# A gated cross-attention and FFN kernel: key projection of the next group ahead of the attention output, late gate loads, and a float32 FFN for the last two groups

## The chip, the cores and the metric

The kernel runs on one core of one Trainium2 chip, as one launch. The metric is the device time of one execution in microseconds. The median before is 78.19 us over three executions.

## The reference

Sixteen batches of 128 rows with 256 features go through one gated attention block and one gated feed-forward block. Cut to what matters:

```python
# x, ctx: (16, 128, 256); mask: (16, 128); all float32
q = layernorm(x) @ Wq.T + bq
k = ctx @ Wk.T + bk
s = where(mask, -inf, q @ k.T)            # per batch, 128 x 128
o = softmax(s) @ ctx                      # the values are ctx itself
x1 = x + tanh(g_xattn) * (o @ Wo.T + bo)
w = (W_ffn >= 0) * 2 - 1                  # signs only
y = clip((layernorm(x1) @ w.T) * scale + bias, -100, 100)
out = x1 + tanh(g_ffn) * y
```

## The kernel before

The sixteen batches are taken as G = 8 groups of GB = 2; L = 7 is the last group. A batch's 128 rows are the partitions and the 256 features are DC = 2 chunks of 128. The two query and key weights are multiplied once into one 256 x 256 product (`multiply_weights`, names `ps_wqk`, `wqk_hi`, `wqk_lo`), so that a group needs only one projection of ctx, called K, against the transposed normalised x. Wo with the gate in it is likewise applied to ctx before the attention, as Z, so that softmax(s) @ Z is already the projected output O.

A group g goes through these steps. TensorE transposes x (`transpose_x`), ctx (`transpose_ctx`) and later x1 (`transpose_x1`). ScalarE evicts the transposed ctx rounded to float32r (`cT_hi`), and VectorE subtracts that from the original to get the rest (`cT_lo`); K and Z are made of three float32r products for each chunk (hi x hi, lo x hi, hi x lo). Scores S are float32. VectorE adds the mask and takes the minimum (`mask_and_min`), ScalarE does the exponential (`exp`), TensorE transposes it (`transpose_p`), ScalarE evicts it, and `attend` multiplies it by Z in float32. VectorE's `residual` divides and adds x with the bias, giving x1. Its statistics (`stats_x1`), its reciprocal standard deviation (`rstd_of_x1`, GpSimd) and its transposed hi and lo halves (`evict_x1T_hi` on ScalarE, `split_x1T` on VectorE) lead to `ffn`, which is eight float32r matmuls of 256 columns for a group. The mean is taken out of the FFN weights (`w_mid`, `wT`). VectorE then scales (`scale_y`), GpSimd adds the bias (`add_bias`), and VectorE clips and adds x1 (`clip_and_add`).

Each engine has its order written out by hand; engines meet by semaphores only, and a wait blocks all that stands behind it on its engine. TensorE's order for group i in the loop is K(i), transposed x1(i-1), Z(i), S(i), transposed ctx(i+1), half of F(i-1), transposed p(i), the other half of F(i-1), transposed x(i+1), O(i). After the loop `finish_last` does the last group with its two batches staggered over spare PSUM banks. The last FFN has hi and lo halves too (`split_last_x1T`), and VectorE finishes it in four steps of two batches each (`scale_last_y`, `add_last_bias`, `clip_last`, `add_last_x1`), behind one addition for the whole of group L-1.

All loads are issued by SP in one order: x(0), Wq, Wk, ctx(0), Wo, x(1), ctx(1), mask, bo, x(2), W_ffn, ctx(2), and so on, each of 256 KB or 128 KB. ScalarE's queue issues bq, bk and the two gates at once at the start. TensorE runs float32 matmuls on zeros (`warm_up`) while it has nothing to do; in the order stand 6, then bq and bk transposed, 3, the gates spread over the partitions, 2, and then the product of weights. ScalarE's first activation is tanh of the gates, and its activation table is loaded ahead of that.

Of the kernel before, what the change touches and what calls it, by code (L numbers as in the profile page):

```python
# [19 lines left out]
def gated_xattn_ffn(nc, x, ctx, mask, g_xattn, g_ffn, wq, bq, wk, bk, wo, bo, w_ffn, scale_ffn, bias_ffn, out):  # L20
# [20 lines left out]
    with ExitStack() as stack:  # L41
# [6 lines left out]
        def bank(name):  # L48
# [12 lines left out]
        last_O, last_F = [ps_O[:, 0], k_bank[:, 0:D]], [ps_F[:, 0], z_bank[:, 0:D]]  # L61
# [29 lines left out]
        wT = sb("wT", [P, DC, D], F32R)  # L91
# [10 lines left out]
        ps_gates = xT_bank[:, 0:2]  # L102
# [15 lines left out]
            sem(n) for n in ("ps_wqk_ready", "wqk_hi_ready", "wqk_lo_ready", "ps_u_ready", "u_ready"))  # L118
        ve_last_done, eps_ready = sem("ve_last_done"), sem("eps_ready")
# [20 lines left out]
        dve_biased_done = sem("dve_biased_done")  # L140
# [5 lines left out]
        def _(sp):  # L146
# [10 lines left out]
            sp.dma_start(wo_sb[:], wo.rearrange("(c p) d -> p c d", p=P)).then_inc(wo_loaded, 16)  # L157
            load_x(1)
            load_ctx(1)
            sp.dma_start(mask_u8[:], mask.rearrange("(o b) k -> o b k", o=1).to_broadcast([P, B, P])  # L160
                         ).then_inc(mask_loaded, 16)
            sp.dma_start(bo_sb[:], bo.rearrange("(o d) -> o d", o=1).to_broadcast([P, D])).then_inc(bo_loaded, 16)
            load_x(2)
# [9 lines left out]
            for g in range(L):  # L173
                if g == L - 2:
                    sp.wait_ge(pool_out_done, GB)
                else:
                    sp.wait_ge(out_done, g + 1 if g < L - 2 else g)
                sp.dma_start(out_rows[:, rows(g), :], out_sb[:, rows(g), :]).then_inc(stored, 16)
            for b in range(GB):
                sp.wait_ge(out_done, L - 1 + b + 1)  # L180
                sp.dma_start(out_rows[:, L * GB + b, :], out_sb[:, L * GB + b, :]).then_inc(stored, 16)
            sp.wait_ge(stored, 16 * (G + 1))

        @block.scalar
        def _(act):
            for k, v in enumerate((bq, bk)):
                act.dma_start(vec_rows[k * DC:(k + 1) * DC, :], v.rearrange("(c p) -> c p", p=P)).then_inc(vecs_loaded, 16)
            for k, v in enumerate((g_xattn, g_ffn)):
                act.dma_start(gate_row[:, k:k + 1], v.rearrange("(o d) -> o d", o=1)).then_inc(gates_loaded, 16)
# [43 lines left out]
            def evict_last_x1T_hi(b):  # L233
                act.wait_ge(x1T_prod, L + b + 1)
                nc.scalar.copy(x1T_hi[:, L % 2, :, b * P:(b + 1) * P], last_x1T[b]).then_inc(x1T_hi_done, 1)
# [9 lines left out]
            for m in range(DC):  # L245
                act.wait_ge(ps_K0_ready, m + 1)
                nc.scalar.activation(K_sb[:, 0, m], ps_K0[m], ACT.Identity, bias=u_col[:, m:m + 1]).then_inc(K_done, 1)  # L247
            act.wait_ge(ps_woT_ready, 1)
            act.wait_ge(tanh_ready, 1)
            nc.scalar.activation(woT_hi[:], by_chunk(z_bank), ACT.Identity, scale=tanh_g[:, 0:1]).then_inc(woT_hi_ready, 1)  # L250
            evict_cT_hi(1)
# [4 lines left out]
            act.wait_ge(w_mean_ready, 1)  # L256
            for c in range(DC):
                nc.scalar.activation(w_mid[:, c], w_sign2[:, c], ACT.Identity, bias=w_mean[:, c:c + 1]).then_inc(w_mid_ready, 1)
            for i in range(1, G + 1):
                if i < G:  # L260
                    evict_K(i)
                if i < G:
                    evict_x1T_hi(i - 1)
                    if i == 1:
                        act.wait_ge(ps_wT_ready, 1)
                        nc.scalar.copy(wT[:], ps_wT).then_inc(wT_ready, 1)
# [546 lines left out]
```

## Time and profile before

| | before |
|---|---|
| median of three executions | 78.19 us (78.17 to 80.32) |
| the profiled execution, its time | 78.39 us |
| its span, first to last instruction | 76.6 us |
| granted TensorE clock, mean over the span | 0.984 |
| TensorE matmul busy | 68.9 us (90%) |
| VectorE busy | 58.9 us (77%) |
| GpSimd busy | 54.7 us (71%) |
| ScalarE busy | 43.2 us (56%) |

The span is that of the profiled execution; 1.8 us of its time lie outside the span. Busy time counts compute only. In the rows further down, PE is TensorE's matmuls (PEld its weight loads), DVE is VectorE, ACT is ScalarE, POOL is GpSimd and SP is SyncE; SPq and ACTq are an engine issuing a DMA. L610 and the like are lines of the kernel. A float32 matmul shows as two records, a float32r matmul as one.

### The profile page before, as it was taken

What the parts mean: (1) busy time and instruction counts of PE and PEld (TensorE: products, weight loads), DVE (VectorE), ACT (ScalarE), POOL (GpSimd) and SP (SyncE); (2) the same over time, 40 slices, a digit from 0 to 9 for tenths busy, and PEclk for the clock granted to TensorE, in tenths of its full rate; (3) what the DMA queues carried; (4) which work ended last, traced back from release to release, by engine and by line L of the source; (5) the groups of instructions that cost most, each with busy time, mean ns of one, the idle gap of its engine ahead of it and who ended that gap; (6) DMA issues with size and microseconds to landing.
All of it is one profiled execution on the core that took longest, in us unless ns stands there. A gap on an engine that the chain in (4) does not pass through costs nothing.

```text
span 76.6 us, 1617 instructions
## 1 busy us (share of the span) xinstructions
PE 68.9 (90%) x513; PEld 64.1 (84%) x513; DVE 58.9 (77%) x186; ACT 43.2 (56%) x118; POOL 54.7 (71%) x111
## 2 busy tenths in 40 slices
PE   4999998989999999999999999999999999975400
PEld 4989997969999999999989999999999899943300
DVE  0191692799437999999899998989877987489980
ACT  0600626775997199619943993597379716726000
POOL 4057008898988998998988798689869338998500
PEclk9999999999999999999999999999999999999985
DMA  0979999999910000040012004000400040012214
GB/s 8 287 223 322 264 248 317 323 368 349 327 56 5 4 4 0 9 137 0 0 42 95 0 0 137 9 0 0 137 0 0 0 137 12 0 59 78 78 59 137
DMA packets 8229, 8.10 MB, mean 106 GB/s; under 512 B 537, under 2 KB 8093, under 8 KB 8221
## 3 DMA queue, kind: packets, MB, share of 16 engines
q1 hardware_dynamic: 8208, 8.00, 33.4%
q8 instruction: 4, 0.07, 0.4%
q14 instruction: 5, 0.03, 0.2%
q10 hardware_dynamic: 12, 0.00, 0.0%
HBM read 5.90 MB, written 2.10 MB: 104 GB/s over the span
## 4 chain that ended last, share of the span: by engine, by line
PE 86%; DVE 4%; ACT 3%; POOLq 1%; issue 1%; POOL 1%; DVEq 0%
PE ps_Z L610 15%; PE ps_K L610 14%; PE ps_S L610 12%; PE ps_F L610 10%; PE ps_O L685 8%; PE ps_xT L605 8%; PE ps_F L730 7%; PE ps_cT L605 5%; PE ps_S L677 3%; POOLq L41 1%; PE ps_O L610 1%; PE ps_O L710 1%; DVE y_biased L484 1%; DVE y_clip L489 1%; ACT Z_sb L215 1%
## 5 line engine op out<-in xcount | busy, mean ns | idle before, releaser
L362 POOL TENSOR_TENSOR xb_sb<-x_sb,bo_g 128x256 f32<-128x256 f32 x16 | 12.9, 829 | 0.6
L367 POOL TENSOR_TENSOR y_biased<-y_scaled,bias_g 128x256 f32<-128x256 f32 x14 | 10.2, 734 | 3.8 <-DVE y_scaled L504 3.8
L210 ACT ACTIVATE K_sb<-ps_K,u_col 128x256 f32<-128x256 f32 x14 | 5.9, 470 | 10.9 <-PE ps_K L610 10.9
L610 PE MATMUL ps_Z<-woT_hi,cT_hi 128*128 128x256 f32 x32 | 9.7, 303 | 0.0
L610 PE MATMUL ps_K<-cT_hi,wqk_hi 128*128 128x256 f32 x30 | 9.7, 323 | 0.0
L610 PE MATMUL ps_F<-wT,x1T_hi 128*128 128x256 f32 x30 | 8.9, 320 | 0.8 <-DVE x1T_lo L472 0.8
L610 PE MATMUL ps_Z<-woT_hi,cT_lo 128*128 128x256 f32 x32 | 9.1, 283 | 0.0
L610 PE MATMUL ps_Z<-woT_lo,cT_hi 128*128 128x256 f32 x32 | 9.0, 283 | 0.0
L610 PE MATMUL ps_S<-K_sb,xT 128*128 128x128 f32 x64 | 8.5, 276 | 0.2 <-ACT K_sb L247 0.2
L610 PE MATMUL ps_K<-cT_hi,wqk_lo 128*128 128x256 f32 x30 | 8.5, 282 | 0.0
L610 PE MATMUL ps_K<-cT_lo,wqk_hi 128*128 128x256 f32 x30 | 8.4, 282 | 0.0
L300 POOL TENSOR_SCALAR ve_x<-mv_x 128x2 f32<-128x2 f32 x8 | 3.1, 386 | 7.2 <-DVE mv_x L412 7.1
L610 PEld LDWEIGHTS ps_S<-K_sb,xT 128*128 128x128 f32 x64 | 7.8, 192 | 0.4 <-issue 0.4
L409 DVE BATCH_NORM_STATS2 bn_x<-x_sb 128x6 f32<-128x256 f32 x16 | 5.9, 408 | 2.5 <-DMA x_sb<-in_x_dram 2.5
L610 PE MATMUL ps_F<-wT,x1T_lo 128*128 128x256 f32 x30 | 7.8, 282 | 0.0
L685 PE MATMUL ps_O<-Z_sb,PT_sb 128*128 128x256 f32 x28 | 7.3, 383 | 0.3 <-ACT PT_sb L227 0.3
L504 DVE SCALAR_TENSOR_TENSOR y_scaled<-ps_F,rstd,scale_g 128x256 f32<-128x256 f32 x14 | 6.5, 474 | 0.7 <-PE ps_F L610 0.7
L424 DVE TENSOR_TENSOR cT_lo<-ps_cT,cT_hi 128x512 fp32r<-128x512 f32 x8 | 5.5, 683 | 1.8 <-ACT cT_hi L193 1.8
L448 DVE SCALAR_TENSOR_TENSOR x_sb<-ps_O,recip_p,xb_sb 128x256 f32<-128x256 f32 x14 | 6.1, 479 | 0.9 <-PE ps_O L685 0.8
L200 ACT ACTIVATE xn<-x_sb,nmr_x,rstd_x 128x256 f32<-128x256 f32 x12 | 6.6, 612 | 0.0
L221 ACT ACTIVATE p_sb<-t_sb,smin 128x128 f32<-128x128 f32 x16 | 6.3, 396 | 0.4 <-DVE smin L437 0.3
L610 PEld LDWEIGHTS ps_F<-wT,x1T_hi 128*128 128x128 f32 x30 | 5.7, 188 | 1.0 <-issue 1.0
(129 smaller groups left out, 206.1 us busy)
## 6 DMA issues: line engine op xcount, KB each, us to landing
x_sb<-in_x_dram SPq DMA_DIRECT2D x8, 256.0 KB, 6.7
ctx_sb<-in_ctx_dram SPq DMA_DIRECT2D x8, 256.0 KB, 6.8
out_dram<-out_sb SPq DMA_DIRECT2D x7, 256.0 KB, 2.1
wq_sb<-in_L_xattn_Wq_dram SPq DMA_DIRECT2D x1, 256.0 KB, 3.0
wk_sb<-in_L_xattn_Wk_dram SPq DMA_DIRECT2D x1, 256.0 KB, 4.3
wo_sb<-in_L_xattn_Wo_dram SPq DMA_DIRECT2D x1, 256.0 KB, 5.2
mask_u<-in_mask_BxS_bk_dram SPq DMA_DIRECT2D x1, 256.0 KB, 6.5
w_sb<-in_L_ffn_weights_dram SPq DMA_DIRECT2D x1, 256.0 KB, 7.8
```

The source lines that it names most:

```text
L200: nc.scalar.activation(xn[:, r], x_sb[:, r], ACT.Identity, scale=rstd_x[:, r:r + 1], bias=nmr_x[:, r:r + 1]).then_inc(xn_done, 1)
L210: nc.scalar.activation(K_sb[:, g % 2, m], ps_K[:, m], ACT.Identity, bias=u_col[:, m:m + 1]).then_inc(K_done, 1)
L221: nc.scalar.activation(p_sb[:, g % 2, b], t_sb[:, g % 2, b], ACT.Exp, scale=-1.0, bias=smin[:, r:r + 1], accum_out=psum_p[:, r:r + 1]).the ...
L362: nc.gpsimd.tensor_tensor(xb_sb[:, r], x_sb[:, r], bo_g[:], ALU.add).then_inc(xb_done, 1)
L367: nc.gpsimd.tensor_tensor(y_biased[:, g % 2, b], y_scaled[:, g % 2, b], bias_g[:, 0], ALU.add).then_inc(biased_done, 1)
L409: nc.vector.bn_stats(bn_x[:, g * GB + b], x_sb[:, g * GB + b]).then_inc(bn_x_done, 1)
L424: nc.vector.tensor_tensor(cT_lo[:, g % 2], ps_cT, cT_hi[:, g % 2].bitcast(F32), ALU.subtract).then_inc(cT_lo_done, 1)
L448: nc.vector.scalar_tensor_tensor(out=x1_sb[:, r], in0=ps_O[:, b], scalar=recip_p[:, r:r + 1], in1=xb_sb[:, r], op0=ALU.mult, op1=ALU.add). ...
L504: nc.vector.scalar_tensor_tensor(out=y_scaled[:, g % 2, b], in0=ps_F[:, b], scalar=rstd_1[:, r:r + 1], in1=scale_g[:], op0=ALU.mult, op1=A ...
L605: last = nc.tensor.transpose(dst[:, c, b * P:(b + 1) * P], src[:, b, c * P:(c + 1) * P], ident[:])
L610: last = nc.tensor.matmul(dst, lhsT, rhs, start=(n == 0), stop=(n == len(pairs) - 1))
L685: last = nc.tensor.matmul(ps_O[:, b], PT_sb[:, g % 2, b], Z_sb[:, g % 2, b], start=True, stop=True)
```

## The change

Seven edits are in it.

1. SP loads Wq, Wk, ctx(0) ahead of x(0), the mask ahead of x(1), and x(2) ahead of bo. ScalarE's queue waits for ctx(0) before it issues the two gate loads.
2. In the prologue the gates' matmul and the two warm-up matmuls behind it are gone from their place. The gates' matmul now stands behind the first half of K(0); x(0) is transposed behind it and the second half of K(0) behind that. ctx(1) is transposed ahead of S(0). VectorE takes the statistics of x(0) behind `wq_neg`.
3. In the loop TensorE's order is K(i), transposed x(i+1), O(i-1), S(i), transposed ctx(i+1), transposed x1(i-1), Z(i), transposed p(i), F(i-1). The other engines' orders follow it; statistics of x are taken three groups ahead.
4. `clip_and_add` is cut in two with `scale_y` between the halves.
5. GpSimd multiplies the FFN weights by the gated scale (`wT_scaled`), a half each in groups 3 and 4.
6. Groups L-1 and L have a float32 FFN on those weights, without hi and lo halves: one ScalarE copy of the transposed x1 and, for each batch, two float32 matmuls of 256 columns. VectorE then multiplies by the standard deviation and adds the bias in one instruction.
7. TensorE's tail is interleaved batch by batch, and the group L-1 is clipped, added and stored last of all.

```diff
-            load_x(0)
             sp.dma_start(wq_sb[:], wq.rearrange("(c p) d -> p c d", p=P)).then_inc(wq_loaded, 16)
             sp.dma_start(wk_sb[:], wk.rearrange("(c p) d -> p c d", p=P)).then_inc(wk_loaded, 16)
             load_ctx(0)
+            load_x(0)
...
+            act.wait_ge(ctx_loaded[0], 16)
             for k, v in enumerate((g_xattn, g_ffn)):
                 act.dma_start(gate_row[:, k:k + 1], v.rearrange("(o d) -> o d", o=1)).then_inc(gates_loaded, 16)
...
-            act.wait_ge(ps_gates_ready, 1)
-            nc.scalar.activation(tanh_g[:], ps_gates, ACT.Tanh).then_inc(tanh_ready, 1)
             act.wait_ge(ps_wqk_ready, 1)
             nc.scalar.copy(wqk_hi[:, 0], ps_wqk[0]).then_inc(wqk_hi_ready, 1)
...
+            act.wait_ge(ps_K0_ready, 1)
+            nc.scalar.activation(K_sb[:, 0, 0], ps_K0[0], ACT.Identity, bias=u_col[:, 0:1]).then_inc(K_done, 1)
+            act.wait_ge(ps_gates_ready, 1)
+            nc.scalar.activation(tanh_g[:], ps_gates, ACT.Tanh).then_inc(tanh_ready, 1)
...
+            for i in range(1, L):
+                evict_K(i)
...
+                evict_xT(i + 1)
+                exp(i)
+                evict_x1T_hi(i - 1)
...
+                evict_cT_hi(i + 1)
+                if i + 2 < G:
+                    normalise_x(i + 2)
+                evict_Z(i)
+                evict_PT(i)
...
+            for i in range(1, L):
+                residual(i - 1)
+                mask_and_min(i)
                 stats_x1(i - 1)
...
                 split_x1T(i - 1)
...
+                split_cT(i + 1)
+                if i >= 2:
+                    clip_y(i - 2)
+                scale_y(i - 1)
+                if i >= 2:
+                    add_x1(i - 2)
+                if i + 3 < G:
+                    stats_x(i + 3)
...
+                nc.gpsimd.tensor_tensor(wT_scaled[:, c], wT[:, c].bitcast(F32), scale_g[:], ALU.mult
+                                        ).then_inc(wT_scaled_ready, 1)
...
             for i in range(1, L):
                 project_K(i)
+                if i == 1:
+
+                    attend(0)
+                    transpose_x(2)
+                else:
+                    transpose_x(i + 1)
+                    attend(i - 1)
+                scores(i)
+                transpose_ctx(i + 1)
                 transpose_x1(i - 1)
...
                 project_Z(i)
...
+                ffn(i - 1)
             project_K(L)
+            attend(L - 1)
+            scores(L)
+            project_last_Z(0)
             transpose_x1(L - 1)
+            transpose_p(L)
+            project_last_Z(1)
+            attend_last(0)
+            ffn_before_last(0)
+            attend_last(1)
+            transpose_last_x1(0)
+            ffn_before_last(1)
+            transpose_last_x1(1)
+            last_ffn(0)
+            last_ffn(1)
...
+                nc.vector.scalar_tensor_tensor(out=y_biased[:, L % 2, b], in0=last_F[b], scalar=rstd_1[:, r:r + 1],
+                                               in1=bias_g[:, 0], op0=ALU.mult, op1=ALU.add).then_inc(last_biased_done, 1)
```

## Rows read from the trace of the kernel before

**Rows 1.** Windows over three of the loop's groups: length, busy time (count) by engine, clock.

```profile
25.20:32.61 7.41, 7.41 (x60) 6.91 (x60) 7.26 (x22) 5.04 (x14) 6.75 (x14) 1.00 0.01 4
32.61:39.91 7.30, 7.30 (x61) 6.90 (x60) 7.04 (x22) 5.03 (x14) 6.71 (x12) 1.00 0.11 36
...
54.52:61.80 7.28, 7.28 (x60) 7.00 (x60) 6.06 (x17) 5.03 (x14) 4.66 (x9) 1.00 0.10 35
```

**Rows 2.** Chain that ended last, one group: start, duration, engine, tile, line, records.

```profile
56.38 1.44 PE ps_Z L610 x12
...
60.49 0.44 PE ps_xT L605 x4
60.93 0.87 PE ps_O L685 x4
```

**Rows 3.** The same chain, the prologue.

```profile
5.74 0.38 PE ps_xT L744 x2
...
6.76 0.87 PE ps_S L610 x4
...
10.15 0.82 PE ps_K L610 x6
...
12.35 1.13 PE ps_S L610 x8
...
15.49 0.58 ACT Z_sb L215
...
16.38 1.10 PE ps_O L685 x4
```

**Rows 4.** Timeline of SP's queue: the third and the fourth load, start and duration.

```profile
1.72 0.46 SPq L155 DMA_DIRECT2D wk_sb<-in_L_xattn_Wk_dram  x1
...
2.22 0.53 SPq L151 DMA_DIRECT2D ctx_sb<-in_ctx_dram  x1
```

**Rows 5.** DMA issues, those two alone: KB each, us from issue to landing.

```profile
wk_sb<-in_L_xattn_Wk_dram SPq DMA_DIRECT2D x1, 256.0 KB, 4.3
...
ctx_sb<-in_ctx_dram SPq DMA_DIRECT2D x1, 256.0 KB, 4.8
```

**Rows 6.** Timeline of ScalarE at the start: its last gate load and the table load.

```profile
1.87 0.27 ACTq L189 DMA_DIRECT2D gate_row<-in_g_ffn_dram  x1
...
2.18 1.28 ACT L238 ACT_TABLE_LOAD   x1 [2.18 <-issue]
```

**Rows 7.** Timeline of VectorE and GpSimd: x(0) from its landing to normalised.

```profile
3.48 0.75 DVE L409 BATCH_NORM_STATS2 bn_x<-x_sb 128x6 f32<-128x256 f32 x2 [2.50 <-DMA x_sb<-in_x_dram]
...
6.39 1.09 POOL L314 TENSOR_SCALAR xn<-x_sb,rstd_x,nmr_x 128x256 f32<-128x256 f32 x2
```

**Rows 8.** Groups by form: count, busy us, mean ns, idle before.

```profile
L221 ACT ACTIVATE p_sb<-t_sb,smin 128x128 f32<-128x128 f32 x16 | 6.3, 396 | 0.4 <-DVE smin L437 0.3
...
L514 DVE TENSOR_TENSOR out_sb<-y_clip,x_sb 128x512 f32<-128x512 f32 x5 | 5.5, 1104 | 0.2
...
L231 ACT CAST x1T_hi<-ps_xT 128x512 fp32r<-128x512 f32 x7 | 4.1, 586 | 0.0
```

**Rows 9.** The chain again, where the scores of the last group have ended.

```profile
65.98 0.95 PE ps_F L610 x8
```

**Rows 10.** Groups by form in the tail, VectorE.

```profile
L589 DVE TENSOR_TENSOR out_sb<-y_clip,x_sb 128x512 f32<-128x512 f32 x1 | 0.7, 680 | 0.0
...
L489 DVE TENSOR_SCALAR y_clip<-y_biased,lim 128x256 f32<-128x256 f32 x2 | 0.7, 404 | 0.0
...
L479 DVE SCALAR_TENSOR_TENSOR y_scaled<-ps_F,rstd,scale_g 128x256 f32<-128x256 f32 x1 | 0.5, 483 | 0.0
```

**Rows 11.** Timeline of VectorE, its last two instructions.

```profile
73.56 0.75 DVE L495 TENSOR_TENSOR out_sb<-y_clip,x_sb 128x256 f32<-128x256 f32 x2
```

**Rows 12.** DMA view, the stores of the output: KB each, median us to landing.

```profile
out_dram<-out_sb SPq DMA_DIRECT2D x7, 256.0 KB, 2.1
...
out_dram<-out_sb SPq DMA_DIRECT2D x2, 128.0 KB, 1.8
```

More of the change, by code:

```diff
@@ L250, in _ @@
             nc.scalar.activation(woT_hi[:], by_chunk(z_bank), ACT.Identity, scale=tanh_g[:, 0:1]).then_inc(woT_hi_ready, 1)
+            act.wait_ge(ps_K0_ready, DC)
+            nc.scalar.activation(K_sb[:, 0, 1], ps_K0[1], ACT.Identity, bias=u_col[:, 1:2]).then_inc(K_done, 1)
             evict_cT_hi(1)
@@ new lines, in _ @@
+            evict_K(L)
+            exp(L)
+            act.wait_ge(x1T_prod, L)
+            nc.scalar.copy(x1T_whole[:], ps_xT).then_inc(x1T_hi_done, 1)
+            evict_PT(L)
+            act.wait_ge(Z_prod, L + 2)
+            nc.scalar.copy(Z_sb[:, L % 2, 1], last_Z[1]).then_inc(last_Z_done[1], 1)
+            for b in range(GB):
+                act.wait_ge(x1T_prod, L + b + 1)
+                nc.scalar.copy(xT[:, 0, :, b * P:(b + 1) * P], last_x1T[b]).then_inc(x1T_hi_done, 1)
+                r = L * GB + b
+                act.wait_ge(mv_1_done, r + 1)
+                nc.scalar.activation(ve_1[:, r:r + 1], mv_1[:, r, 1:2], ACT.Identity, bias=eps_col[:, 0:1]
+                                     ).then_inc(ve_last_done, 1)
@@ L501, in scale_y @@
                 dve.wait_ge(F_prod, g + 1)
-                for b in batches:
+                for b in range(GB):
                     r = g * GB + b
@@ L686, in attend, with ffn @@
                 last.then_inc(O_prod, 1)
-            def ffn(g, batches):
+            def ffn(g):
                 pe.wait_ge(x1T_lo_done, g + 1)
@@ L693, in ffn @@
                     pe.wait_ge(wT_ready, 1)
-                for b in batches:
+                for b in range(GB):
                     pairs = []
@@ new lines, in ffn, with project_last_Z @@
+                last.then_inc(F_prod, 1)
+            def project_last_Z(b):
+                pe.wait_ge(Z_done, L)
+                if b == 1:
+                    pe.wait_ge(K_done, DC * G)
+                pairs = []
+                for c in range(DC):
+                    c_hi, c_lo = (t[:, L % 2, c, b * P:(b + 1) * P] for t in (cT_hi, cT_lo))
+                    pairs += [(c_hi, woT_hi[:, c]), (c_hi, woT_lo[:, c]), (c_lo, woT_hi[:, c])]
+                accumulate(last_Z[b], pairs).then_inc(Z_prod, 1)
@@ new lines, in ffn_before_last, with attend_last @@
+            def ffn_before_last(b):
+                pe.wait_ge(x1T_hi_done, L)
+                pe.wait_ge(wT_scaled_ready, DC)
+                pe.wait_ge(scaled_done, GB * (L - 1))
+                last = accumulate(ps_F[:, b], [(x1T_whole[:, c, b * P:(b + 1) * P], wT_scaled[:, c]) for c in range(DC)])
+                if b == GB - 1:
+                    last.then_inc(F_prod, 1)
+            def attend_last(b):
+                pe.wait_ge(last_Z_done[b], 1)
+                pe.wait_ge(PT_done, GB * L + b + 1)
+                if b == 0:
+                    pe.wait_ge(x1_done, GB * L)
+                nc.tensor.matmul(last_O[b], PT_sb[:, L % 2, b], Z_sb[:, L % 2, b], start=True, stop=True
+                                 ).then_inc(O_prod, 1)
@@ new lines, in transpose_last_x1, with last_ffn @@
+            def transpose_last_x1(b):
+                pe.wait_ge(x1_done, GB * L + b + 1)
+                for c in range(DC):
+                    last = nc.tensor.transpose(last_x1T[b][:, c], x1_sb[:, GB * L + b, c * P:(c + 1) * P], ident[:])
+                last.then_inc(x1T_prod, 1)
+            def last_ffn(b):
+                pe.wait_ge(x1T_hi_done, L + b + 1)
+                pe.wait_ge(wT_scaled_ready, DC)
+                accumulate(last_F[b], [(xT[:, 0, c, b * P:(b + 1) * P], wT_scaled[:, c]) for c in range(DC)]
+                           ).then_inc(F_prod, 1)
```

292 lines of the change are left out of this document (109 added, 183 removed).

## The prediction, made before the change was run

> **What bounds the kernel now.** I read the windows over the loop's groups first. In the last of three shown TensorE is busy 7.28 us of 7.28, in the first 7.41 of 7.41 [rows 1]: it has no hole, so a reordering can take nothing out of a group. VectorE is nearly as full, 7.26 of 7.41 and 7.04 of 7.30 us in the groups that also carry the statistics of a later x and the final add; without the statistics it is at 6.06 of 7.28 [rows 1]. So a new wait on VectorE of more than 0.2 to 0.3 us lengthens such a group. The chain that ended last says the same: one TensorE piece after another, each at a fixed price [rows 2]. Only the two ends are left to win something: the prologue up to the first O, where TensorE once stands behind ScalarE's evictions of Z and p [rows 3], and the tail behind the scores of the last group, which end at 65.98 [rows 9], 76.6 - 65.98 = 10.6 us before the end.
>
> **Start.** The product of weights starts at 6.76; the gates' matmul starts at 5.74 and it and the warm-up behind it are all that lies between [rows 3], so the product can start about 1.0 us sooner, at 5.74, if Wk is there. The third load in the queue lands at 1.72 + 4.3 = 6.0 and the fourth at 2.22 + 4.8 = 7.0 [rows 4, 5]. Wk is now second and so surely there by 6.0, ctx(0) is third (6.0), x(0) fourth (7.0, not first). What was won is then waited away, by two chains.
>
> Chain A is x(0). From the first look at x(0), 3.48, to its last normalised row, 6.39 + 1.09 = 7.48, are 4.0 us [rows 7], and that latency moves with the load: 7.0 + 4.0 = 11.0. Before, it ended at 7.48 and was hidden under the weights; now it is behind them. Behind it stand: x(0) transposed, 0.44 [rows 2]; the second half of K(0), half of a 12-record projection, 0.72 [rows 2]; the gates' matmul in front of it all, up to 0.38 [rows 3]; and ScalarE's eviction of half of K with two hand-overs, for which I take 0.6 (an eviction of 512 columns is 0.59, of 128 columns 0.40 [rows 8]). With half of the gates' price that is 11.0 + 0.2 + 0.44 + 0.72 + 0.6 = 13.0 for the first scores.
>
> Chain B is ScalarE. Its gate loads wait for ctx(0), 6.0; two issues take 0.6 (one is 0.27, and the table load began 0.31 after the start of the last [rows 6]); and the table load of 1.28 us stands behind them in its order, since it comes ahead of the first activation [rows 6]. Before, that was over at 3.46, in idle time. Now it would run 6.6 to 7.9, and the first eviction of the product waits for it, though the product is ready at about 6.6. From the product's first half (7.63) to K(0) (10.15) were 2.5 us [rows 3], so K(0) starts at 10.4 at the latest and its half ends at 11.1 or 11.2, about when x(0) is ready. So B is hidden by A, with nothing to spare. The product at 5.74 could also meet the clock at 1.2 GHz rather than 2.4: twice its 0.87 [rows 3] still ends before 7.9. Bounds for the first scores: 12.4 (loads that land 0.6 sooner) and 13.4 (the full gates' price and 0.2 for each chain's hand-overs); I take 13.0, against 12.35 before [rows 3].
>
> The scores are 0.65 later. But ctx(1) is already transposed, -0.44 (as [rows 2]), and K(1) now lies ahead of O(0), in the place where TensorE waited for the evictions of Z and p. From Z(0)'s end, just before 15.49, to the end of that O, 16.38 + 1.10 = 17.48, are 2.0 us [rows 3], and the work in it is 0.44 (p), 0.44 (x) and 0.87 (O) [rows 2] = 1.75 at the most: -0.3. Start in all: +0.65 - 0.44 - 0.3 = **-0.1** (from -0.7 to +0.3).
>
> **Loop.** TensorE does the same pieces. Their prices don't change, and the five groups took 7.28 to 7.41. The new order has one thin place. F(i-1) needs the low half of x1, which VectorE computes when ScalarE has evicted the high half; and ScalarE does that behind both exponentials. From the start of `mask_and_min` this is about 0.3 + 2 x 0.40 + 0.59 = 1.7 us [rows 8], or 1.8 with the reads of the sums between. VectorE arrives there sooner, at 0.6 (two masks) + 0.9 (two statistics) = 1.5 us, my reading from half-lengths of the same kind (0.75 for two statistics [rows 7]), and stands idle for 0.3. Added to its 7.04 us of work [rows 1] this is 7.34, 0.06 above TensorE's 7.28. That concerns groups 2, 3 and 4, which carry both the statistics of x and the final add: 3 x 0.06 = 0.2. The others have 1 us to spare on VectorE. Before, the first groups lost 0.15 to 0.2 as well (7.41 against 7.28). I take **+0.1**; the bounds are 0 and +1.0, which is 0.33 for three groups: 7.26 [rows 1] + 0.35. Splitting clip and add costs nothing by itself, as it is the same two instructions; the two scalings of weights on GpSimd (about 0.8 us each by the same shape) fall in groups 3 and 4, where it is busy 6.7 of 7.3 [rows 1], and what they delay there (bias and norm of a later x) has about 1 us of slack; without that cover they cost 0.2 each.
>
> **Tail.** Counted from the end of the last scores, TensorE now does Z(7) 1.44, x1(6) transposed 0.44, p(7) 0.44, O(7) 0.87, F(6), x1(7) transposed 0.44, and F(7). Four records of float32 with 256 columns take 0.87 (O), thus 0.44 for a matmul [rows 2]; the float32r FFN of a group was 0.95 [rows 9]. In float32 it is four matmuls, 1.74: the change makes TensorE 0.8 us slower in each of the two groups, and pays it for the VectorE split between. The sum is 1.44 + 0.44 + 0.44 + 0.87 + 1.74 + 0.44 + 1.74 = 7.1 us, without a hole as the batches are interleaved and every eviction (0.4 to 0.6 [rows 8]) has 0.7 or more of other work over it. F of the first batch is ready at 7.1 - 0.87 = 6.2. VectorE then needs 0.48 + 0.40 + 0.40 for a batch, now one dependent chain, and twice: 6.3 + 1.3 + 1.3 = 8.9; and the add of the whole group 6, 0.68, comes last: 9.6 [rows 10]. From VectorE's last result, 73.56 + 0.75 = 74.31 [rows 11], to the end were 2.3 us; the last store is now 256 KB and not 128 KB, 2.1 against 1.8 [rows 12], so 2.6. The tail is 12.2 us against 10.6, +1.6. But Z(7) and x1(6) transposed, 1.88 together, came before the last scores and now come behind: **-0.3** (-0.6 without the larger store and with a free group add; +0.4 if VectorE's instructions stretch beside GpSimd's clips as the add did, 1.10 against 0.68 [rows 8, 10]).
>
> **Sum.** -0.1 + 0.1 - 0.3 = -0.3 us on a span of 76.6. The profiled execution is 78.39, 0.2 above the median; so the median goes from 78.19 to **77.9 us**.
>
> **Two rules of the Trainium skill against this.** The trace has the table load at 1.28 us with nothing in front of or behind it that waits [rows 6]. ScalarE: Activation LUTs in the Trainium skill, section What ACT_TABLE_LOAD costs, has the same 1283 ns and adds about 1380 ns of drain; this trace can't show it, and by it chain B would end 1.4 us later and the median be near 79.1. The final add on VectorE took 1.10 us in the loop and 0.68 in the tail [rows 8, 10]. The page Perfetto Trace Analysis of the Trainium skill, section Optimizing Scalar/DVE Operations, says that GpSimd and VectorE share an SBUF read port; the trace agrees with it, and it speaks for the slower rival below.
>
> **The rivals.**
> - *The table load holds ScalarE longer than its own row.* The activation behind it starts up to a second 1.28 later. Chain B then sets the start: first scores at 14.2 to 14.3, the rest as above, 77.9 + 1.2 = 79.1. For it: the load has been moved out of idle time. Against: in the trace nothing stood behind it, so nothing shows such a cost.
> - *The loop waits on VectorE.* This is the side of slower. F(i-1) waits for the low half of x1 in every group, because VectorE's adds stretch beside GpSimd; VectorE is at 7.26 + 0.35 = 7.6 [rows 1], 0.3 for each of the six groups, +1.8: 79.6. It decides from 0.05 for a group on: 6 x 0.05 eats the 0.3 of the forecast. For it: the first group of before, 7.41. Against: the later groups carry less.
> - *The start is really shorter.* Loads land sooner with x(0) out of the way, and the table load runs in ScalarE's wait for ctx(0), so neither chain holds TensorE; the 1.0 us of warm-up is won whole, first scores at 12.0: 76.9. For it: the warm-up stood on the path. Against: 4.0 us of latency of x(0) [rows 7] don't go away.
> - *The float32 FFN gives nothing back.* The tail is as long as the sum of both, 77.9 + 0.8 = 78.7; it needs a hole in TensorE's tail of 0.8, and all operands are ready earlier in my walk.
>
> **Chances.** Forecast 0.50, table load 0.12, VectorE's loop 0.14, shorter start 0.18, tail 0.06. The forecast's own range is 77.2 to 78.6 (start and tail at their bounds against each other). With the rivals the range is 76.7 to 79.3: it leaves out half of the loop's case and a third of the short start. About 2% is what a measurement of this kernel can tell from no change, 76.6 and 79.8. Faster than that needs the short start and a good tail (0.12); slower needs the loop's case beyond 79.6 or two of them (0.09).
>
> **What would show it.** In the profile after: x(0) normalised at about 11 and the first scores at 13.0; a table load at 6.6 that ends at 7.9, and the distance of the next activation from it; windows over a group at 7.3 us with TensorE full; a wait of TensorE in front of F for `x1T_lo` if the loop's case holds; four float32 FFN matmuls at 1.74 for groups 6 and 7; and some 12.2 us from the end of the last scores to the end. The prediction is wrong first of all if the loads don't land in the order and at the times of their slots.

## The result, and the profile after

| | before | after |
|---|---|---|
| median | 78.18 us (78.00 to 80.32) | 80.02 us (79.05 to 82.72) |
| ratio to before, 95% interval | | 1.0134 (1.0086 to 1.0182) |
| the profiled execution, its time | 78.39 us | 79.05 us |
| its span | 76.6 us | 77.2 us |
| granted TensorE clock, mean | 0.984 | 0.982 |

Two of the four executions of after (80.76 and 82.72) had a lower mean granted clock (0.965 and 0.950); the ratio leaves these two and the slow one of before (80.32) out, and by it the change costs 1.0 us, where the forecast was a gain of 0.3. Two repetitions in later sessions, on two chips, gave 1.0108 (1.0011 to 1.0205) and 1.0059 (1.0016 to 1.0101). So the change makes the kernel some 0.5 to 1 us longer; in the two profiles the span is 0.6 us longer.

The chain that ended last, of after, from the third load to O(0), and two pieces of group 1 behind it, S(1) and F(0) (start, duration, engine, tile, line, records). The names are those of the PSUM banks: ps_O at 11.21 is the gates' matmul, ps_F at 12.18 the second half of K(0), and ps_S with two records the transposed p.

```profile
1.71 4.33 DMA ctx_sb<-in_ctx_dram
...
6.33 4.84 DMA gate_row<-in_g_ffn_dram
...
11.21 0.38 PE ps_O L779 x2
11.59 0.59 PE ps_xT L614 x4
12.18 0.73 PE ps_F L619 x6
...
13.55 1.13 PE ps_S L619 x8
...
18.21 0.87 PE ps_O L694 x4
...
19.52 1.12 PE ps_S L619 x8
...
23.60 0.95 PE ps_F L619 x8
```

The first scores start at 13.55, against 12.35 before [rows 3], and neither x(0) nor the table load is in the chain: it is the load of the second gate, one number, which ScalarE issued at 6.33, with SP's loads of 256 KB under way, and which landed at 11.17. ScalarE's timeline shows the table load beside it:

```profile
6.63 1.28 ACT L239 ACT_TABLE_LOAD   x1 [6.63 <-DMA ctx_sb<-in_ctx_dram]
7.92 0.37 ACT L239 CAST wqk_hi<-ps_S 128x256 fp32r<-128x256 f32 x1
```

Windows over two of the loop's groups of after, the partners of [rows 1]:

```profile
24.55:31.91 7.36, 7.36 (x61) 7.04 (x60) 5.74 (x20) 5.02 (x17) 6.12 (x13) 1.00 0.02 4
...
53.94:61.28 7.34, 7.34 (x61) 7.03 (x60) 5.49 (x17) 4.36 (x14) 4.80 (x8) 1.00 0.11 36
```

A group takes 7.34 to 7.36 us. TensorE looks full, but VectorE is at 5.5 to 5.7 in these two and at 6.3 to 6.4 in the three groups between them, not at 7. The view of waits says what TensorE's full time hides (who <- for whom: us in total, times, longest):

```profile
DVE x1T_lo L452 <- ACT x1T_hi L236: 1.9, 6, 0.3
...
PEld ps_F L619 <- DVE x1T_lo L452: 1.0, 5, 0.2
```

And the end of the chain, from the last group of the loop on (cf. [rows 9]):

```profile
59.88 0.22 PE ps_S L686 x2
60.10 1.18 PE ps_F L619 x8
61.28 1.44 PE ps_K L619 x12
62.72 0.87 PE ps_O L694 x4
63.59 0.11 issue
63.70 1.13 PE ps_S L619 x8
...
70.14 0.88 PE ps_S L619 x4
```

F(5) has 1.18 where F took 0.95 before [rows 9]; in front of the scores of group 7 TensorE stands; and the last piece shown, which is the FFN of the first batch of group 7 (it lies in the bank of the scores), ends at 71.02.

**Where the time went.** I cut both spans at the same work. To the end of K(1) and O(0): before 17.49 + 1.43 = 18.9 (O(0) from [rows 3], a K as in the loop), after 19.08: +0.2. From there to the start of K(7), which is 61.80 before [rows 1] and 61.28 after, are 42.9 before; less the O(6) that the new order does later, 0.87 [rows 2], that is 42.0, against 42.2 after: +0.2. From there to the end: before 14.8 with that O added 15.7, after 15.9: +0.25. Sum +0.6, the difference of the spans.

### The profile page after: what moved, and what is told of

Same layout as the page of the kernel before. It is cut to its first block, busy times and chain, and to the rows that moved or that the text cites. A ratio compares the mean times of both kernels' runs of the same rounds, so it can differ in the third digit from the quotient of the medians.

```text
span 77.2 us, 1595 instructions
## 1 busy us (share of the span) xinstructions
PE 69.7 (90%) x509; PEld 65.1 (84%) x509; DVE 55.9 (72%) x182; ACT 42.4 (55%) x118; POOL 54.5 (71%) x111
## 4 chain that ended last, share of the span: by engine, by line
PE 76%; DMA 12%; DVE 3%; issue 2%; SPq 1%; DVEq 1%; ACT 1%; ACTq 0%
PE ps_K L619 14%; PE ps_Z L619 14%; PE ps_F L619 12%; PE ps_S L619 11%; PE ps_xT L614 9%; PE ps_O L694 8%; DMA gate_row<-in_g_ffn_dram 6%; DMA ctx_sb<-in_ctx_dram 6%; PE ps_cT L614 3%; PE ps_S L686 2%; DVE y_biased L497 1%; DVE y_clip L500 1%; PE ps_O L733 1%; DVEq L41 1%; ACT K_sb L252 1%
## 5 line engine op out<-in xcount | busy, mean ns | idle before, releaser
L382 POOL TENSOR_TENSOR y_biased<-y_scaled,bias_g 128x256 f32<-128x256 f32 x12 | 9.4, 802 | 0.2
L619 PE MATMUL ps_Z<-woT_hi,cT_hi 128*128 128x256 f32 x30 | 9.1, 304 | 0.0
L619 PE MATMUL ps_K<-cT_hi,wqk_hi 128*128 128x256 f32 x30 | 8.7, 289 | 0.5 <-DVE wqk_lo L547 0.5
L619 PE MATMUL ps_Z<-woT_hi,cT_lo 128*128 128x256 f32 x30 | 8.5, 283 | 0.0
L306 POOL TENSOR_SCALAR ve_x<-mv_x 128x2 f32<-128x2 f32 x8 | 1.8, 220 | 7.9 <-DVE mv_x L435 7.7
L512 DVE SCALAR_TENSOR_TENSOR y_scaled<-ps_F,rstd,scale_g 128x256 f32<-128x256 f32 x12 | 5.3, 479 | 2.4 <-PE ps_F L619 2.4
L619 PE MATMUL ps_F<-wT,x1T_hi 128*128 128x256 f32 x24 | 6.6, 307 | 0.0
L619 PEld LDWEIGHTS ps_K<-cT_hi,wqk_hi 128*128 128x128 f32 x30 | 5.7, 191 | 0.7 <-DVE cT_lo L447 0.7
L308 POOL TENSOR_TENSOR rstd_x<-ve_x,minus_half 128x2 f32<-128x2 f32 x8 | 5.7, 713 | 0.7
L619 PE MATMUL ps_F<-wT,x1T_lo 128*128 128x256 f32 x24 | 6.0, 282 | 0.0
```

Source lines behind the costliest of these rows:

```text
L308: nc.gpsimd.tensor_tensor(rstd_x[:, rows(g)], ve_x[:, rows(g)], minus_half[:], ALU.pow).then_inc(rstd_x_done, 1)
L382: nc.gpsimd.tensor_tensor(y_biased[:, g % 2, b], y_scaled[:, g % 2, b], bias_g[:, 0], ALU.add).then_inc(biased_done, 1)
L512: nc.vector.scalar_tensor_tensor(out=y_scaled[:, g % 2, b], in0=ps_F[:, b], scalar=rstd_1[:, r:r + 1], in1=scale_g[:], op0=ALU.mult, op1=A ...
L619: last = nc.tensor.matmul(dst, lhsT, rhs, start=(n == 0), stop=(n == len(pairs) - 1))
```

## The experiments

All kernels but the repetitions differ from after by the diff shown, and those whose expectation speaks of early gates by that edit as well. "First scores" is the start of S(0), and "from K(7)" counts from the start of that projection, both in the profile. Each ratio is to before, measured with it in the same session; the four sessions of experiments ran on four chips.

### Gates early

```diff
-            act.wait_ge(ctx_loaded[0], 16)
             for k, v in enumerate((g_xattn, g_ffn)):
```

> The changed kernel without ScalarE's wait for ctx(0) ahead of the two gate loads; all else is kept. Theory 'late gates': in the changed kernel the gates landed at 11.17 us and held TensorE behind the first half of K(0). With early gates the first scores start at 12.8 instead of 13.55 and the span falls by 0.7, from 77.2 to 76.5. Theory 'late x': x(0) is normalised only at 10.75 and sets the start anyway; the scores come 0.2 to 0.3 sooner and the span falls by 0.2 at most.

Ratio 1.003 (0.9999 to 1.0061). The chain of that profile starts with x(0):

```profile
2.23 5.28 DMA x_sb<-in_x_dram
...
10.38 1.11 POOL xn L319 x2
...
13.57 1.13 PE ps_S L618 x8
```

x(0) landed at 7.51 here and at 6.8 in the profile of after, and normalised 4.0 us behind its landing, as forecast; so here my chain A sets the start, at 13.57, and no gate is waited for. The load of x(0) landed 0.7 us later here than there, and that is as much as the price in question. The ratio is 1.0% under that of after, but it is from another session. I took both up again below.

### Table load early, gates late

```diff
+            act.wait_ge(zeros_ready, 1)
+            nc.scalar.copy(act_first[:], zeros[:, 0:1])
             act.wait_ge(ctx_loaded[0], 16)
```

> The changed kernel with one tiny activation ahead of ScalarE's wait for ctx(0), so that the activation table is loaded in idle time while the gates still come late. Theory 'late gates': nothing is won, as the gates land at 11.2 as before, the first scores start at 13.55 and the span is 77.2 within 0.1. Theory 'table load': the eviction of the product starts at 7.0 instead of 7.92, K(0) starts at 9.4 instead of 9.98 and the span falls by 0.5.

Ratio 1.0067 (1.0009 to 1.0125), first scores at 13.49, the gates again last, at 11.11. With the table load out of the way K(0) starts at 9.74 and not at 9.98, but the gates hold TensorE all the same, and the first scores move by 0.06 us. So the table load does not set this start. That it holds ScalarE no longer than its own row is shown by the 0.01 us between its end and the next activation in the rows above, and the rival of the table load is refuted.

### The whole start of before

```diff
+            load_x(0)
             sp.dma_start(wq_sb[:], ...)
             sp.dma_start(wk_sb[:], ...)
             load_ctx(0)
-            load_x(0)
...
+            pe.wait_ge(gates_loaded, 32)
+            pe.wait_ge(ones_ready, 1)
+            nc.tensor.matmul(ps_gates, ones_row[:], gate_row[:], start=True, stop=True).then_inc(ps_gates_ready, 1)
+            warm_up(2)
             pe.wait_ge(wk_loaded, 16)
```

(and gates early, tanh first on ScalarE, statistics of x(0) first on VectorE)

> The changed kernel with the whole start of before: loads in the old order, gates at once, their matmul and warm-up ahead of the weights, x(0) transposed ahead of K(0), ctx(1) behind the scores. First scores at 12.35 again. Theory 'the start costs': K(1) and O(0) end at 18.6 instead of 19.08 and the span falls by 0.5. If only the late gates are at fault, this is no better than early gates alone: both within 0.2 of each other. Theory 'the loss is in the loop and tail': the span stays at 77.2 within 0.2.

Ratio 1.0035 (0.9993 to 1.0078): no different from gates early alone. Its first scores started at 12.98, as Wk, now third, landed at 7.08. So the start's other edits together show no price beside early gates that these intervals (0.3 to 0.4% to either side) can tell; in the two profiles the order of x(0), Wq, Wk and ctx(0) moves the lateness from one load to another.

### FFN of the last two groups in float32r again

```diff
-            nc.scalar.copy(x1T_whole[:], ps_xT).then_inc(x1T_hi_done, 1)
+            nc.scalar.copy(x1T_hi[:, (L - 1) % 2], ps_xT).then_inc(x1T_hi_done, 1)
...
+            split_x1T(L - 1)
             last_x1(0)
...
-                accumulate(last_F[b], [(xT[:, 0, c, b * P:(b + 1) * P], wT_scaled[:, c]) for c in range(DC)]
+                accumulate(last_F[b], [(t[:, L % 2, c, b * P:(b + 1) * P], wT[:, c]) for c in range(DC)
+                                       for t in (x1T_hi, x1T_lo)]).then_inc(F_prod, 1)
```

> The changed kernel with the FFN of the last two groups in float32r with hi and lo halves of x1 again (its output leaves out the scale in these two groups, so that the instructions behind it are the same). TensorE has 1.6 us less work behind the last scores, VectorE 1.5 us more. Theory 'TensorE sets the tail': the end comes 0.8 to 1.6 us sooner. Theory 'VectorE and the hand-overs set the tail': the split halves take back what TensorE wins, the span moves by 0.2 at most.

Ratio 1.0212 (1.0167 to 1.0258), but in its profile the gates landed at 12.30 and the first scores are at 14.69, 1.1 later than after's: that is nearly all of the 1.3 us on the span (78.5). Two of its three executions in the ratio also had a granted clock of 0.965 and 0.966. So the ratio says nothing of the tail, which is told by the chain:

```profile
64.85 1.13 PE ps_S L628 x8
...
70.46 0.44 PE ps_cT L749 x2
70.89 0.71 PE ps_S L628 x4
```

From the end of the last scores, 65.98, to the end are 12.5 us, against 12.4 in after: TensorE has some 1.6 us less of matmuls (an FFN of a group 0.95 instead of 1.73), and the hole opens in front of the transposed x1 (70.46), which waits for VectorE. So the float32 FFN is about free where it stands, as forecast, and saves VectorE three splits (0.69, and 0.42 twice); it doesn't gain more than 0.1. That is read from one profile of each.

### The changed kernel once more, and the wait in the loop

> The changed kernel once more, beside the kernels of this call. Theory 'late gates': over many executions it stays 0.6 to 0.9 us slower than the same kernel with early gates. Rival 'the landings of that one chip and hour': beside them it is within 0.3 us of early gates.

Ratio 1.0108 (1.0011 to 1.0205); its profile had x(0) landing at 8.3 and then a granted clock of 0.5 for a while (the transposed x(0) took 1.12 us), and can't be compared line by line.

The suspect of the loop is the wait of F for the low half of x1. It can be taken away without a new buffer: ScalarE evicts the transposed x1 between the two exponentials (with gates early).

```diff
-                exp(i)
-                evict_x1T_hi(i - 1)
+                exp_of(i, 0)
+                evict_x1T_hi(i - 1)
+                exp_of(i, 1)
```

> Early gates, and in the loop ScalarE evicts the transposed x1 between the two exponentials instead of behind both. Theory 'F waits for ScalarE's order': the high half comes 0.4 us sooner, the wait of 0.24 in front of F goes, p's transposes pay 0.16 of it back, and a group takes 7.28 instead of 7.34: 0.4 us over six groups, from the first scores to the end 63.3 instead of 63.7. Theory 'VectorE is full': the low half comes no sooner, and groups stay at 7.34.

Ratio 0.9922 (0.9886 to 0.9958), span 75.5: faster than before and than after. Windows over the same two groups:

```profile
23.94:31.06 7.12, 7.12 (x60) 7.01 (x60) 5.76 (x20) 5.12 (x15) 5.88 (x13) 1.00 0.02 5
...
52.44:59.56 7.12, 7.12 (x60) 7.01 (x60) 5.62 (x18) 4.83 (x15) 5.08 (x8) 1.00 0.12 39
```

and the chain at the place of the wait:

```profile
58.38 0.22 PE ps_S L689 x2
58.59 0.97 PE ps_F L622 x8
```

Groups 2 to 6 are 0.22 to 0.24 shorter each, those without statistics or final add too (I had expected 7.28). From the first scores, 12.92, to the end are 62.6 us, against 63.65 in after: 1.1 us. And 7.12 is below before's 7.28. So the new order has a floor of its own that is 0.16 lower, and after gave all of it back in the wait, and a little more.

### Z(7) ahead of the last scores

```diff
-            scores(L)
             project_last_Z(0)
+            scores(L)
```

> Early gates, and in the tail the first half of Z(7) ahead of the last scores, so that it lies over ScalarE's eviction of K(7). Theory 'the exposed eviction of K(7) costs 0.35': the 0.35 us of stall in front of the last scores goes and the end comes 0.3 sooner (63.4 from the first scores to the end). Rival 'the exponentials are next': the scores themselves come 0.4 later, p(7) is late and TensorE waits there instead; within 0.1 of 63.7.

Ratio 1.0063 (1.0021 to 1.0106), 0.3% above gates early alone, which the intervals don't tell apart. The chain:

```profile
63.67 0.87 PE ps_O L693 x4
64.54 0.71 PE ps_Z L618 x6
65.25 0.46 PE ps_S L618 x4
...
66.18 0.89 ACT p_sb L225 x4
...
67.12 0.33 PE ps_S L685
```

This profile had a granted clock of 0.5 for a while in its start, and full clock in the tail, so I compare from K(7) on: 16.1 us, against 15.9 in after. The stall in front of the scores is gone, and the same time is lost one step on, where the transposed p now waits for the exponentials: the rival. K(7)'s eviction is exposed, but covering it with work that delays the scores gained nothing here.

### O(0) ahead of K(1)

```diff
-                project_K(i)
-                if i == 1:
-                    attend(0)
+                if i == 1:
+                    attend(0)
+                project_K(i)
```

> Early gates, and O(0) ahead of K(1) again as in the kernel before, later groups unchanged. Theory: K(1) covers ScalarE's evictions of Z(0) and p(0), so undoing it brings back a stall of 0.3 to 0.4 us in front of O(0), and from the first scores to the end are 64.0 to 64.1. Rival: the covered stall only moved to the scores of group 1, which begin 0.2 us late in the changed kernel; then it is 63.7 to 63.8.

Ratio 1.0135 (1.0062 to 1.0207), 1.0% above gates early.

```profile
15.75 0.59 ACT Z_sb L219
...
16.64 1.10 PE ps_O L693 x4
...
19.61 0.54 issue
20.14 1.13 PE ps_S L618 x8
```

O(0) again waits for the eviction of Z, as in [rows 3], and K(1)'s eviction comes out from under O as well (0.54): neither my theory (0.3 to 0.4) nor its rival had both. From the first scores to K(7) are 48.8 us, against 47.7 in after. K ahead of O is thus worth 1.0 us in the first group by the new order's own measure, where I had taken 0.3: it is the good part of the change.

### The final add of group 6 before batch 1, and x1 between the exponentials with late gates

```diff
             finish_last_y(0)
-            finish_last_y(1)
...
             nc.vector.tensor_tensor(out_sb[:, rows(L - 1)], y_clip[:, (L - 1) % 2], x1_sb[:, rows(L - 1)], ALU.add
                                     ).then_inc(out_done, 1)
+            finish_last_y(1)
```

(on top of early gates and x1 between the exponentials; SP's last stores follow in the same order)

> Early gates and the eviction of the transposed x1 between the exponentials (span 75.5 us, median 77.84), and one edit more: VectorE does the final add of group 6 between the two batches of group 7, so that the last store is one of 128 KB and not one of 256 KB. Theory that the last store's size sets the end: 0.3 us less (1.8 against 2.1 us of landing), about 77.5. Rival: GpSimd's two clips of group 6 are not done by then and VectorE waits for them, or its adds stretch beside them; then the end is the same or up to 0.3 later, 77.8 to 78.1.

Ratio 0.9849 (0.9809 to 0.9889), median 77.06: the fastest version, together with the last one below. VectorE's end, in the chain:

```profile
71.05 0.68 DVE out_sb L608
...
72.60 0.43 DVE out_sb L507
```

VectorE ends at 73.03, 2.2 us before the end of the span, and a store of 128 KB is the last; in after it ends at 74.67, and 2.5 us follow. From K(7) to the end the profile has 15.55 us, against 15.94 with x1 between the exponentials alone: 0.4 us.

The kernel with the eviction between the exponentials and the gates still late:

> The changed kernel with one edit: ScalarE evicts the transposed x1 between the two exponentials of a group instead of behind both. The gates stay late (their loads wait for ctx(0)). With the gates early this edit brought 62.6 us from the first scores to the end instead of 63.7. My theory is that the start and the loop are independent: here too 62.6 us from the first scores to the end and groups of 7.12 us, but first scores at 13.5 as in the changed kernel, when its gates land at about 11.2; span 76.1, median about 78.0 in quiet executions, 0.3 to 0.8 above the kernel with early gates. The rival: the late gates cost nothing by themselves, x(0) sets the start just the same, and the median is that of the kernel with early gates within 0.2 (77.8). Which of the two loads stands last ahead of the gates' matmul and the transposed x(0) in the profile decides.

Ratio 0.991 (0.9871 to 0.9948). By the ratio it can't be told from 0.9922 with early gates, as the rival says. Its profile has the gates landing last, at 12.40, and TensorE waiting 1.25 us for them, as my theory says, but at a granted clock of 0.5 behind it, so that it gives no price. As the two ratios were from different chips I put the question again, at the end.

### K(7) ahead of F(5)

```diff
                 transpose_p(i)
+                if i == L - 1:
+                    project_K(L)
                 ffn(i - 1)
-            project_K(L)
```

> The kernel before this one (early gates, eviction between the exponentials, final add of group 6 first) with one edit more: TensorE does K(7) ahead of F(5) instead of behind it. In the changed kernel TensorE stands 0.35 us in front of the scores of group 7, as only O(6), 0.87 us, lies between K(7) and them, and ScalarE's eviction of K is not done. Theory: with F(5) over the eviction too the stall of 0.35 us (0.11 as the chain names it, the rest inside the gap between the pieces) goes and the end comes 0.2 to 0.35 earlier. Rival: the next thing is late by as much, either the low half of ctx(7) in front of K(7), or F(5) and with it VectorE's work on group 5; then no gain.

Ratio 1.0072 (1.0045 to 1.0098), 2.3% above the kernel that it edits. The rival by far:

```profile
59.44 0.70 DVE cT_lo L451
...
60.18 1.70 PE ps_K L622 x12
...
63.80 0.91 issue
...
65.30 0.47 DVE x_sb L475
...
66.02 0.89 ACT p_sb L225 x4
```

K(7) waits for the low half of ctx(7). O(6) now stands behind both K(7) and F(5), and VectorE, whose order puts the residual of group 6 ahead of the mask of group 7, waits for O(6) (the 0.91), so that the exponentials of group 7 end at 66.9 and the transposed p stands behind them. From the first scores (13.89) to the end (77.7) are 63.8 us, against 62.55 in the kernel that it edits: for the 0.35 us it pays 1.25. The exposed eviction is the cheapest of the places tried.

### The price of the late gates, on one chip

Three repetitions in one session, and the load order once more:

> The changed kernel once more, beside the two below on the same chip. If the late gates cost something by themselves it stands 0.5 to 0.8 us above the kernel with early gates, and its profile has the gates landing at about 11.2 and the gates' matmul waiting for them; if the difference was one of chips and sessions it stands within 0.2 of it, at 78.6 to 78.9.

> The changed kernel with the gates' loads issued at once, once more: 78.6 as in the first session. Late gates with a price: 0.5 or more below the changed kernel. Late gates without one: the same as the changed kernel within 0.2.

> Late gates and the eviction of the transposed x1 between the exponentials, once more: 1.1 us below the changed kernel, since the start is the same and the loop loses its wait; about 77.9 if the late gates have their price, 77.6 if they have none.

Ratios: the changed kernel 1.0059 (1.0016 to 1.0101), gates early 1.0025 (0.999 to 1.0059), x1 between with late gates 0.9952 (0.9915 to 0.9989). So the late gates cost about 0.3% or 0.27 us, half of what I expected at the least, and the two intervals overlap: by these executions their price is small and may be nothing. The wait in the loop costs 1.07%, 0.8 us, and there the intervals don't overlap. Why so little, when the first scores start at 12.95 in the profile with early gates and at 13.62 in the last one with late gates, 0.67 us apart? ScalarE's timeline shows it at x(2), first with the gates early:

```profile
17.37 1.09 ACT L204 ACTIVATE xn<-x_sb,nmr_x,rstd_x 128x256 f32<-128x256 f32 x2 [0.40 <-POOL nmr_x L311]
```

then with them late, in the profile of after:

```profile
17.59 1.09 ACT L205 ACTIVATE xn<-x_sb,nmr_x,rstd_x 128x256 f32<-128x256 f32 x2
```

The normalised x(2) hangs on GpSimd's factors. With the gates early ScalarE waits 0.40 us for them, the transposed x(2) takes TensorE 0.65 instead of 0.44 us, and 0.11 of waiting stands ahead of S(1): 0.35 of the 0.67 us is waited away again, and K(7) starts 48.1 us behind the first scores, against 47.7 in after. The first profile with early gates had x(0) later and no such wait, and there it is 47.7 as well.

```diff
-            load_ctx(0)
             load_x(0)
+            load_ctx(0)
```

> The fastest kernel so far (early gates, eviction between the exponentials, final add of group 6 first; 77.06) with one edit: x(0) is loaded third and ctx(0) fourth. Theory that x(0) sets the start: it lands 0.5 sooner; TensorE stood 0.38 us before the transposed x(0) in that profile, so first scores 0.3 to 0.4 sooner, about 76.7. Rival: ctx(0) is now the late one; its transposition stands between the halves of the product of weights, and everything behind waits, so first scores the same or up to 0.5 later, 77.1 to 77.6.

Ratio 0.9856 (0.9815 to 0.9898), the same as the kernel that it edits (0.9849, on another chip).

```profile
2.22 4.89 DMA ctx_sb<-in_ctx_dram
...
7.16 0.66 PE ps_cT L617 x4
```

ctx(0) is the late one now, at 7.12, and the first scores are at 12.94: the rival. The fourth of the four loads landed 4.9 us behind its issue here, and with x(0) in that place 4.3 to 6.1 us in the other profiles; the first scores need all four.

## Why the prediction was wrong

Three steps failed: the landing of the late gates and the last eviction of K were put at nothing, and in the loop I took TensorE's pieces at fixed prices and charged the wait for the low half of x1 to VectorE's load instead of setting it against TensorE's work in between.

**The start (forecast -0.1, measured +0.2).** Chain A held as a length (4.0 us from x(0)'s landing to its normalised row; in after 10.75, forecast 11.0), chain B held within its bounds (the table load 6.63 to 7.91, K(0) at 9.98 against 10.4 at the latest). The step that failed is one that I did not cost: I gave the gates' matmul its 0.38 us and asked only when ScalarE could issue the gates' loads, not when they land. [rows 6] has the last one issued at 1.87, and the matmul had its data at 5.74 or sooner [rows 3]; at 6.33 the same one number took 4.84 us. No run issues a gate late without the big loads, so what made it long is not shown, only that it lands late. Its landing at 11.17 stands 0.4 behind the normalised x(0), and its matmul's 0.38 comes on top. The first scores are 0.55 later than forecast; the stretch from them to the end of K(1) and O(0) gives back 0.3 more than forecast, mostly by the transposed p at 0.22 and not 0.44, and by Z(0) at 1.44 where before had 1.54. The experiments put the net price of the late gates at about 0.27 us.

**The loop (forecast +0.1, measured +0.2).** The number is nearly right, by luck, and its reason is not. I had the times of the hand-over right:

```profile
57.61 0.28 DVE L460 CUSTOM_DVE_ANT_0 t_sb<-ps_S,mask_add 128x128 f32<-128x128 f32 x1
...
58.73 0.56 ACT L236 CAST x1T_hi<-ps_xT 128x512 fp32r<-128x512 f32 x1
...
59.32 0.69 DVE L452 TENSOR_TENSOR x1T_lo<-ps_xT,x1T_hi 128x512 fp32r<-128x512 f32 x1 [0.33 <-ACT x1T_hi L236]
```

ScalarE is done 1.7 us after the masks began (forecast 1.7) and VectorE idles 0.33 (forecast 0.3). But I charged that idle time to VectorE's load, in the three groups where it was full. What it costs is a latency: the low half is ready at 60.01, 2.4 us after the scores ended, and TensorE has only 0.44 + 0.44 + 1.43 + 0.22 = 2.53 us of work in between (57.58 to 60.10), and the low half stands only 0.09 ahead of the end of that: F's weight load starts at 60.07, behind an idle time of 0.20 put down to the low half, and F takes 1.18. I never set these two sums against each other; with my 0.44 for the transposed p they would have read 2.75 against 2.4 and would have looked safe. So it is 0.22 to 0.24 for each of F(1) to F(5), the five waits of the view above. F(0) has the transposed FFN weights, 0.44, as cover besides, took 0.95 and shows no wait. This is the place of my slower rival, but not its mechanism, since VectorE is at 5.5 to 6.4 of 7.3.

The second error hid the first. "Their prices don't change" is wrong, and with it "a reordering can take nothing out of a group": the transposed p takes 0.22 ahead of a whole F, and took 0.38 between its halves before, so the new order's group is 7.12, not 7.28. Five times +0.23 and six times -0.16 is +0.2. Two smaller things cancel: S(1) took 1.12 and not 0.89, as ScalarE, which normalises x(2) first, has K(1) evicted only at 19.40; and before had 0.2 of irregular pieces, most of it in its first full group, whose 7.41 is 0.13 above 7.28 (I wrote 0.15 to 0.2).

The slower rival's other leg fell as well: the final add on VectorE took 1104 ns in the loop of before [rows 8] and takes 681 ns in after. I had said that splitting clip and add costs nothing, and it pays: in before each of the five adds starts while a long GpSimd instruction is under way (since 30.36 for the first add, at 30.60), while in after the add stands behind `scale_y` and begins 0.06 to 0.09 us ahead of the long GpSimd instruction beside it (32.81 against 32.88). In the fastest version the adds start with 0.23 to 0.36 us of a GpSimd instruction still to run, and take 0.77 to 0.89. No run tests that order by itself.

**The tail (forecast -0.3, measured +0.25).** The walk behind the last scores was good in its sums. From the end of the last scores to the end: forecast 12.2, measured 12.4; F of the first batch ready after 6.2, measured 71.02 - 64.83 = 6.19; VectorE's last result after 9.6, measured 9.8:

```profile
71.11 0.48 DVE L497 SCALAR_TENSOR_TENSOR y_biased<-ps_S,rstd,bias_g 128x256 f32<-128x256 f32 x1 [0.20 <-PE ps_S L619]
...
72.10 0.66 DVE L503 TENSOR_TENSOR out_sb<-y_clip,x_sb 128x256 f32<-128x256 f32 x1
...
73.99 0.68 DVE L606 TENSOR_TENSOR out_sb<-y_clip,x_sb 128x512 f32<-128x512 f32 x1
```

The 6.19 is partly luck: the transposed p took 0.22 and not 0.44, and the two matmuls of O(7) in front of that F took 0.63 and 0.43, 0.2 more than the 0.87 that I had. The 0.2 on VectorE's end is 0.66 for the first add instead of 0.43, and hand-overs of 0.03 in a chain that depends on itself. GpSimd's clips run from 71.37 to 72.49 beside that add; this agrees with Perfetto Trace Analysis in the Trainium skill, section Optimizing Scalar/DVE Operations, by which the two engines share a port. What failed is where I began to count. In the loop 0.44 (transposed x) + 0.87 (O) lie between K and the scores; for group 7 there is no further x, and the 0.87 alone does not cover ScalarE's two evictions of K with the hand-overs before and behind them: TensorE stands 0.11, and the scores take 1.13 and not 0.89, together 0.35 us more. I had walked behind the last scores only, and put this wait at nothing.

**The rivals.** The table load: refuted; the first activation behind it starts 0.01 us later, and the added drain of ScalarE: Activation LUTs in the Trainium skill, section What ACT_TABLE_LOAD costs, isn't seen in this trace. The float32 FFN that gives nothing back: not borne out; with a float32r FFN in its place the tail is 0.1 us longer, so the float32 form is no loss. The short start: refuted by the landings, with first scores at 13.55 and not at 12.0. None of my cases had the small gates' load as its mechanism, nor the last eviction of K.

By size: of the 0.9 us between forecast and measured span, 0.26 is the start, 0.1 the loop, 0.35 the eviction of K(7), and 0.2 VectorE's end. And 0.8 us by the ratios of one session, 1.1 us by the profiles, could be had in the loop by the order of two instructions on ScalarE.

## What to carry to other kernels

A group in which TensorE is "full" can still wait: its records stretch over the wait, so compare the duration of each piece between places (0.97 against 1.18) and read the list of waits for the weight loads. When an order is changed, write down for every hand-over the latency of the other engines and, against it, the sum of TensorE's work that lies between, in the last group separately, because there pieces are missing from the cover; how busy the waiting engine is did not decide it here. And for a small DMA that is issued later than before, cost its landing (here up to 5.8 us on) and not its issue.

## What the runs showed of the hardware

- A load of one number issued at 1.87 was there when asked for, at 5.74 at the latest; issued between 5.8 and 6.8, while SP's 256 KB loads were under way, it took 4.4 to 5.8 us in the six profiles where it stands in the chain. The same 256 KB load in the same slot, x(0) as the fourth, took 4.3 to 6.1 us in profiles of kernels with the same first four loads; its landing alone moves the first scores by as much as the edits of the start.
- The transposed p, two records, took 0.38 us between the two halves of F and 0.22 between Z and F.
- The granted clock can fall in the start of the changed kernel. In the windows of one of its repetitions the stretch behind the gates' landing reads (length, busy PE, PEld, DVE, ACT, POOL, clock, DMA):

```profile
11.20:13.50 2.30, 1.91 (x10) 1.90 (x11) 0.82 (x4) 1.28 (x3) 1.50 (x5) 0.64 1.08 285
```

TensorE stood 0.88 us before K(0) and 0.54 before the gates there, and from 12.0 to 15.0 the granted clock is 0.50, which is 1.2 GHz (x(0) transposed took 1.05 us in the chain, 0.59 in after). In after it stood 0.49 and 0.28 and kept 2.4 GHz. The length of these holes does not decide by itself: with the float32r tail TensorE stood 0.56 and 1.01 and kept 2.4 GHz. Nor do early gates keep the clock up: the profile of Z(7) ahead of the last scores, with holes of 0.49 and 0.39 us, has 0.50 from 11.4 to 13.8. But it is rarer with them. Of the 55 executions of the kernels with late gates 23 had a mean granted clock of 0.97 or less, of the 80 with early gates 5, of 29 of before none. In the session on one chip the medians over all executions are 79.43 for the changed kernel and 78.46 with early gates, 1.0 us apart where the ratios say 0.27. Why the clock falls more often with late gates wasn't tested.
